# A top-k threshold search with its last count merged into the picking of candidates, in a sparse-adjacency and mixture-of-experts kernel on one core

## The reference, cut to what matters

```python
sim = jnp.einsum('bhnd,bhmd->bnm', Q, K) / (jnp.sqrt(jnp.float32(d)) * H)
k = max(1, int(n * TOP_K_RATIO))            # 153 of 512
threshold = jax.lax.top_k(sim, k)[0][:, :, -1:]
A_learned = jax.nn.sigmoid(sim) * (sim >= threshold)
A_learned = (A_learned + jnp.swapaxes(A_learned, -1, -2)) * 0.5
x = x + tanh(g_xattn) * ((1.0 - gamma) * layernorm(x) + gamma * A_learned)

probs = softmax(layernorm(x) @ gate_w)      # 8 experts, the best 2 of each token
h = gelu(einsum('th,ehi->eti', xn, fc1_w) + fc1_b)
y = einsum('eti,eih->eth', h, fc2_w) + fc2_b
x = x + tanh(g_ffn) * einsum('eth,te->th', y, combine)
```

## Time and profile before

| | |
|---|---|
| three runs | 392.31 us median (389.15 to 394.56) |
| the profiled execution | 393.13 us |
| its span on the core | 391.4 us |
| PE busy | 340.3 us (87%) |
| PE weight loads | 243.9 us (62%) |
| DVE busy | 214.4 us (55%) |
| ACT busy | 167.8 us (43%) |
| POOL busy | 109.3 us (28%) |

### The profile page before, as it was taken

The page is one execution under the profiler, slowest core; times in us unless marked ns, Lnnn a source line. Parts: engine busy times, 40 slices in busy tenths (PEclk is TensorE's granted clock), DMA queues, the critical chain, the costliest instruction groups (busy, mean ns, idle before and its releaser), DMA issues.

```text
span 391.4 us, 6052 instructions
## 1 busy us (share of the span) xinstructions
PE 340.3 (87%) x1867; PEld 243.9 (62%) x1867; DVE 214.4 (55%) x761; ACT 167.8 (43%) x372; POOL 109.3 (28%) x150
## 2 busy tenths in 40 slices
PE   4942358987999999989999899999999999999960
PEld 3310148667696768758786676876888673949520
DVE  0587888777798787688888458173142111120110
ACT  2357735746528366665547812421223222222220
POOL 5020000062013273231226411237413133413233
PEclk9695565698999999999999999999999999999995
DMA  3999999996456766757517775558797657445364
GB/s 112 359 198 342 392 387 386 386 378 199 82 124 173 190 180 146 164 92 186 128 38 197 173 138 137 160 87 229 143 200 158 125 103 153 74 74 102 55 97 54
DMA packets 56517, 69.48 MB, mean 178 GB/s; under 512 B 10112, under 2 KB 29856, under 8 KB 56480
## 3 DMA queue, kind: packets, MB, share of 16 engines
q1 hardware_dynamic: 48416, 50.63, 43.3%
q0 software_dynamic: 8064, 18.42, 24.8%
HBM read 40.61 MB, written 28.42 MB: 176 GB/s over the span
## 4 chain that ended last, share of the span: by engine, by line
PE 53%; issue 21%; DMA 9%; DVE 5%; POOL 4%; POOLq 3%; another core or an unknown queue 1%; DVEq 1%; ACT 1%; ACTq 0%
PE ps L1703 21%; PE ps L1678 15%; PE ps L1688 11%; DMA out_rows<-ys,dst 7%; PE ps L1713 3%; DMA out_rows<-ab,dst 3%; POOL xs_rows L535 2%; PE ps L1641 2%; PE ps L1621 1%; PE ps L1633 1%; POOLq L521 1%; POOL out_rows L549 1%; POOL out_rows L561 1%; POOLq L500 1%
## 5 line engine op out<-in xcount | busy, mean ns | idle before, releaser
L1678 PEld LDWEIGHTS ps<-xgT_r,weights 128*128 128x128 f32 x768 | 89.5, 195 | 6.0 <-issue 5.9
L1678 PE MATMUL ps<-xgT_r,weights 128*128 128x128 f32 x768 | 91.3, 279 | 1.7 <-issue 1.7
L1703 PE MATMUL ps<-weights,act_r 128*128 128x512 f32 x192 | 87.7, 605 | 0.9 <-ACT act_r L743 0.9
L549 POOL DMA_INDIRECT out_rows<-ys,dst x24 | 38.6, 1608 | 116.9 <-DMA out_rows<-ys,dst 60.3
L1703 PEld LDWEIGHTS ps<-weights,act_r 128*128 128x128 f32 x192 | 35.7, 193 | 39.7 <-issue 38.4
L1688 PEld LDWEIGHTS ps<-sim,weights 128*128 128x128 f32 x256 | 41.9, 190 | 2.4 <-issue 2.2
L1688 PE MATMUL ps<-sim,weights 128*128 128x192 f32 x256 | 42.4, 326 | 0.0
L743 ACT ACTIVATE act_r<-ps,b1T 128x128 f32<-128x128 f32 x96 | 27.3, 367 | 32.9 <-PE ps L1678 31.7
L674 ACT ACTIVATE ab<-sim,t_now 128x512 bf16<-128x512 f32 x44 | 31.3, 715 | 19.9 <-DVEq L1050 10.0
L535 POOL DMA_INDIRECT xs_rows<-ab,pos x32 | 32.0, 1001 | 24.5 <-DVEq L1216 15.6
L750 ACT ACTIVATE ys<-ys,meta 128x512 f32<-128x512 f32 x24 | 17.2, 722 | 39.0 <-DVE ys L1293 35.9
(11 more groups left out here) (187 smaller groups left out, 443.8 us busy)
## 6 DMA issues: line engine op xcount, KB each, us to landing
weights<-in_L_ffn_fc_w SPq DMA_DIRECT2D x16, 1024.0 KB, 14.7
b_r<-in_L_ffn_fc_b SPq DMA_DIRECT2D x32, 256.0 KB
xg_r<-xs_rows SPq DMA_DIRECT2D x88, 64.0 KB
xb<-in_x SPq DMA_DIRECT2D x4, 1024.0 KB, 7.6
out_rows<-xb SPq DMA_DIRECT2D x4, 1024.0 KB
xs_rows<-ys SPq DMA_DIRECT2D x3, 1032.0 KB, 12.3
sim<-xs_rows SPq DMA_DIRECT2D x32, 96.0 KB
xs_rows<-ys SPq DMA_DIRECT2D x1, 2064.0 KB, 21.3
```

The source lines that it names most:

```text
L549: pool.indirect_dma_start(out=out_rows, out_offset=bass.IndirectOffsetOnAxis(ap=dst[:, k % 2, e:e + 1], axis=0), in_=result_rows(m), in_of ...
L1678: mm = pe.matmul(ps[:, n % 2, i * P:(i + 1) * P], weights[:, e, 0, h, i * P:(i + 1) * P], rows[:, h * P:(h + 1) * P], start=(h == 0), stop ...
L1703: mm = pe.matmul(ps[:, 2 + m % 2, :], rows, weights[:, e, 1, i, :], start=(i == 0), stop=(i == IB - 1))
```

## The change

**One round less.** `ROUNDS` is 3. In the last `narrow` a new trial `t_now` is still made; where the count at `hi` is already near enough (at most 8 above the wanted place), `hi` is taken in its stead. ACT then does one Sign with a row sum for each tile (`candidates`), which is the count of that trial and the marking of the values above it at once. DVE's `largest` multiplies the sign by 3e38 and takes the minimum with the scores. `prepare_pick` is gone; what it did moves into `threshold`, which works with the new count.

**Batch 0 first.** Batch 0's sign tiles lie in `xg_r` and `x1T` instead of `ab`, so that `squash(0, t)` and `halve(0, t)` can run before the search ends, straight after the scores. ACT's first instruction is the copy of `m_qk`, and the coefficients (which need a DMA) come after `context(0)`. On all engines statistics, scales and counts of batches 1 to 3 stand later, behind batch 0's next steps. `affine_x(0)` stands after the search.

**TensorE.** `keep_busy` loops: 24, 12 and 36 before; now 24 at the start, 36 once two tiles of batch 0 have been through `largest` (`BUSY_SEARCH`), 48 after its proof (`BUSY_MASK`), 20 between the second and the third adjacency tile (`BUSY_ADD`), 12 (`BUSY_ROWS`). The order of layers and batch steps is rewritten.

**DMA.** `fc1` and `fc2` of an expert have a semaphore each. Expert 0's weights are asked for ahead of the zeros; those of expert 2 and later each wait until `fc1` of the expert before has landed; experts 6 and 7 stand behind the store of x1(0) and the load of x(2). Zeros are written to 32 slots before each window's end instead of 64.

The core of the diff (the rewritten orders are shown behind it by the instruction lists):

```diff
-ROUNDS = 4
+ROUNDS = 3
-BUSY_LOADS, BUSY_MASK, BUSY_ROWS = 24, 36, 12
+AHEAD = 6
+BUSY_LOADS, BUSY_SEARCH, BUSY_MASK, BUSY_ADD, BUSY_ROWS = 24, 36, 48, 20, 12
         def penal(b, t):
+            if b == 0:
+                return xg_r[:, t, :] if t < 2 else x1T[:, t - 2, :]
             return ab[:, b % 2, t, 0:SEQ]
+            def load_weights(e):
+                if e >= 2:
+                    sp.wait_ge(fc1_in[e - 1], 16)
+                sp.dma_start(weights[:, e, 0], fc1[e].rearrange("(k p) n -> p k n", p=P)).then_inc(fc1_in[e], 16)
+                sp.dma_start(weights[:, e, 1], fc2[e].rearrange("(k p) n -> p k n", p=P)).then_inc(fc2_in[e], 16)
+            load_weights(0)
             sp.wait_ge(consts, 1)
-            for first, n in [(at - HALF, HALF) for at in CLOSED[:-1]] + [(CAP - P, P)]:
+            for first, n in [(at - SHORT, SHORT) for at in CLOSED[:-1]] + [(CAP - P, P)]:
...
-            for e in range(E):
-                sp.dma_start(weights[:, e, 0], fc1[e].rearrange("(k p) n -> p k n", p=P)).then_inc(fc_in[e], 16)
-                sp.dma_start(weights[:, e, 1], fc2[e].rearrange("(k p) n -> p k n", p=P)).then_inc(fc_in[e], 16)
+            for e in range(1, AHEAD):
+                load_weights(e)
             store_x1(0)
+            load_weights(6)
             load_x(2)
+            load_weights(7)
             load_meta(0)
-            def above(b, t):
+            def candidates(b, t):
                 i = b * BT + t
                 act.wait_ge(trial[b], ROUNDS + 1)
-                act.activation(penal(b, t), score_of(b, t), ACT.Relu, bias=hi_big[:, i:i + 1],
-                               scale=BIG).then_inc(pen_done, 1)
+                act.activation(penal(b, t), score_of(b, t), ACT.Sign, bias=t_now[:, i:i + 1], scale=-1.0,
+                               accum_out=cnt[:, i:i + 1]).then_inc(pen_done, 1)
             def squash(b, t):
-                act.wait_ge(pen_used, b * BT + t + 1)
+                if b == 0:
+                    act.wait_ge(sim_sb, t + 1)
+                else:
+                    act.wait_ge(pen_used, b * BT + t + 1)
                 if r == ROUNDS - 1:
-                    dve.tensor_scalar(hi_big[:, at], hi[:, at], -BIG, None, ALU.mult)
-                    dve.drain().then_inc(trial[b], 1)
-                    return
+                    dve.tensor_tensor(under[:], n_hi[:, at], near[:, at], ALU.is_le)
...
+                if r == ROUNDS - 1:
+                    dve.drain()
+                    dve.copy_predicated(t_now[:, at], under[:], hi[:, at])
                 dve.drain().then_inc(trial[b], 1)
             def largest(b, t):
-                dve.tensor_tensor(penal(b, t), score_of(b, t), penal(b, t), ALU.subtract)
+                dve.scalar_tensor_tensor(penal(b, t), penal(b, t), BIG, score_of(b, t), ALU.mult, ALU.min)
             def threshold(b):
                 dve.drain()
-                dve.tensor_tensor(pick[:], pick[:], top[:], ALU.mult)
+                dve.tensor_scalar(pick0[:], cnt[:, at], 0.5, TOPK - 1 - SEQ / 2, ALU.mult, ALU.add)
...
+            def busy_to_threshold():
+                pe.wait_ge(pen_used, 2)
+                keep_busy(BUSY_SEARCH)
```

591 lines of the change are left out of this document (279 added, 312 removed).

## The result

The change made the kernel slower by more than a third: 542.98 us median (541.92 to 543.62), beside 390.73 us for the kernel before on the same chip, a ratio of 1.387 (1.376 to 1.399). The forecast was 381. The profiled execution has a span of 541.9 us, against 391.4.

A forecast was written before the change was run, and what follows sets the result against it. TensorE's work bounds from the first layer at 92.2 us, batch 0's DVE and ACT chain before it. Batch 1's first layer 10.8 earlier plus 0.9 of adjacencies gives 11.7 off, less 0.3 for waits: 381.0 us, range 375 to 391.

The forecast's parts named there:

- the search does not do what it says: Rival: one unproved row of 512 sends DVE into the slow loop, over 100 us a batch; chance 0.02.
- The path to the first layer: Batch 0's chain of search, mask, gate and places: first expert layer at 79.4 to 83.3 instead of 92.22.
- the stall: At the end of expert 1's picking, before the first layer: ACT idle 4.75 us before; half of it again gives 81.4.
- The low clock at the turns and gates: Batch 0's turns and gates on TensorE stay at clock 0.50 as before; `best_two` starts at 63.4, 10.1 us earlier.
- From there to batch 1's rows: From the first layer to layer1(1, 0): it starts at 150.5 instead of 161.28, set by batch 1's rows.
- proof(1) at 100.8: Batch 1's proof on DVE, after 28 us of work from one_hot(1)'s end at 71.7, plus 1 of waits.
- plus 1 of waits: DVE's waits between one_hot(1)'s end and batch 1's proof, taken as 1 us on 28 us of work.
- best_two(1) at 125.5: Batch 1's best two behind its gates, after mask done at 107.1 and last add at 116; places at 131.5.
- the transfers' part: DMA order of weights and fewer blank rows: weights are there in time, fewer zeros "only helps"; no gain counted.
- 63 of 70 us: DVE's work between first layer and layer1(1, 0), 55.7 before: near to being the bound.
- batch 1's rows come late: Rival: POOL's five adds of 9.3 end at 141, layer1(1, 0) at 159.5, time 390; range 386 to 392, chance 0.17.
- Behind `layer1(1, 0)`: Rest of the kernel after batch 1's first layer: the gain carries to the end, rows of batches 2 and 3 in time.

The follow-up runs named there:

- e2_one_row: Changed kernel, with the slow loop entered only from two unproved rows on, leaving a single one with a wrong threshold: 389.99 us in one run.
- e1_nudge: Changed kernel, with the last narrow handing over hi * (1 + 2^-22) instead of hi: 393.45 us, 1.0031 times the kernel before.
- e10_both: e1_nudge with the edits of e5_root_first and e8_filler together: 0.9974 times the kernel before.
- e5_root_first: e1_nudge with GpSimd taking batch 1's root ahead of batch 0's fourth add instead of behind it: 0.9966 times the kernel before.
- e6_transfers: e1_nudge with 64 blank rows a batch and the weights asked for together behind them and the batch inputs, as before: 402.67 us, ratio 1.0278.
- e15_scatter_late: e10_both with batch 2's scatter moved behind two more adds and a root on GpSimd: 1.0102 times the kernel before.
- e9_behind: e1_nudge with other work put ahead of the ScalarE and VectorE instructions that wait for layer1(1, 5): 1.0032 times the kernel before.
- e12_list64: e10_both with 64 more filling matmuls in TensorE's wait at 17.9 to 25.4, written out one by one: 0.9977 times the kernel before.
- e8_filler: e1_nudge with 72 filling matmuls instead of 20 ahead of batch 0's third adjacency tile: 1.0005 times the kernel before.

## Why the prediction was wrong

**The step that failed.** The rival "the search does not do what it says" had the loop in it, with its place and price ("over 100 us a batch"; 1.86 us for a pair and its idle time, not 1.4, makes it 141, and 147.7 with the copies and the last MAX8 of each tile), and got a chance of 0.02 on this ground: "the same trials are made as before, and `hi` is taken under the same condition; no row of the loop is in the trace". By the code the first three trials are made as before. But what is done at `hi` is not the same. Before, the candidates were made at `hi` by Relu, and the count that went with them was `n_hi` from an earlier round, which on the tiles that VectorE counts comes from a compare (`is_le`), a whole number even where a score equals `hi`; and a fourth trial could still replace `hi`. Now every tile is counted once more at `hi` by Sign, and the sum must be a whole count. Of 2,048 rows one was enough (e2_one_row, with the trace of the changed kernel), and a shift of one part in four million took it away (e1_nudge). By the code a tie on a tile that ScalarE counts would have left a half in `n_hi` before too, so which of the two differences it was depends on the row's tile, and of that only is known that it is not tile 3. The trace of the kernel before could not have shown it: it shows times, and this hung on values.

**The path to the first layer** was right. First sign 17.67 (forecast 16.8), candidates 31.01 (29.5), mask 41.59 (40.2), last add 54.1 + 0.7, 13.2 behind the mask's start (13.25), `best_two` 64.30 (63.4), first layer 82.39 (between 79.4, without the stall, and 83.3, with it in full). The first sign was off by 0.9 us, and the wait for `scores(1, 0)` ahead of the candidates (2.16 us) was in no term. The low clock at the turns and gates came as forecast, and the sum holds there, with one reading in it that was short: before, `best_two` began 11.1 us behind the last add (62.34 to 73.51), and the forecast took 9.9, where the gates end; 9.5 were measured.

**From there to batch 1's rows**, 150.5 against 159.29 in e1_nudge, two terms of the sum were mis-sized. "proof(1) at 100.8" was 105.32: "plus 1 of waits" on VectorE was 2.66 for the places of batch 0 alone, a wait that grows when batch 0 gets earlier (7.30 in e10_both). "best_two(1) at 125.5" was 134.59 in e1_nudge; of the 4.6 us added there, the root behind an indirect add is 3.3 (e5_root_first). Besides, the transfers' part stood at nothing in the sum and is worth 9.7 us (e6_transfers); that did the forecast no harm, since the part is in the changed kernel and helps, and this was luck. The warning that VectorE would have 63 of 70 us to do missed too: from 80 to 150 it was busy for 52.37 in e1_nudge, so its waits made it late, more than its work did. The rival "batch 1's rows come late" has the right numbers (159.5 and 390 us) for the kernel without the loop, but not its mechanism: it had GpSimd's adds last until 141, and in e1_nudge GpSimd was through with them at 132.0 and stood idle for 8.90 us, waiting for VectorE:

```profile
140.92 1.02 POOL L550 DMA_INDIRECT xs_rows<-ab,pos  x1 [8.90 <-DVEq L1220]
```

**Behind `layer1(1, 0)`** the forecast let 11 us pass through untouched. In e1_nudge more than the 2.0 us that remained stands in TensorE's wait of 4.91 us for the late event, with the slower matmuls behind it. Under the same scatter (206.8 to 217.1) TensorE had only two waits before, of 0.63 and 1.06 us, until 218.27 and 219.69. That this is what used up the 2.0 us is argued from the rows; e15_scatter_late, meant to show it, put another wait in its place.

**What stays open.** How a scatter delays TensorE's event, and what that costs, was not found: it is not the engines that wait (e9_behind) and not the place in TensorE's list (e12_list64). That the unproved row's count is a half was argued, not read, and its tile is not known. What brings the low clock of TensorE where it hardly waits (e8_filler at 60.7) is open too.
